# Channel-major LayerNorms, an early query product and gates broadcast through DRAM in a conv, attention and mixture-of-experts kernel

## What is computed

```python
# conv block
y = depthwise_conv3x3(ln(x) @ inproj.T + b)          # ln over the 64 channels of a point
s = [y rows forward, backward, y columns forward, backward]      # 4 token orders
r = ln(s) @ ssm_in.T + b; a, g = split(r); u = a * sigmoid(g)
ys = nan_clean(conv1d_3taps(u) @ ssm_out.T + b) + s
x1 = nan_clean(mean_of_4_orders(ys) @ outproj.T + b) + x
# attention block, t = tokens of x1
xa = ln(t); q, k, v = split(xa @ W_qkv.T + b)        # 16 heads of 4 channels
k, v = head_ln(k), head_ln(v)
out = q @ (k.T @ v / 256)                            # per image and head
t2 = t + gelu((out + xa) @ W_proj.T + b) + xa
# mixture of experts: 8 experts, 64 -> 256 -> 64, the two best are weighed by softmax
xf = ln(t2); w = softmax of the top two logits of xf @ Wg + bg
result = t2 + sum_e w[:, e] * (gelu(xf @ W1[e] + b1[e]) @ W2[e] + b2[e])
```

## Time and profile before

| | |
|---|---|
| median of 3 runs | 100.32 us (100.15 to 100.49) |
| the profiled execution's own time | 100.63 us |
| its span, first to last instruction | 98.9 us |
| busy PE, DVE, ACT, POOL | 87.7, 67.8, 55.1, 25.0 us |

### The profile page before, as it was taken

One profiled execution on the slowest core, in us unless ns is written; L12 is line 12 of the kernel. 1 busy time (PEld: TensorE's weight loads), 2 busy tenths in 40 slices (PEclk: granted clock), 3 DMA queues, 4 the chain that ended last, 5 costly groups with the idle time before them and its releaser, 6 DMA issues. The chain is left out here.

```text
span 98.9 us, 1512 instructions
## 1 busy us (share of the span) xinstructions
PE 87.7 (89%) x445; PEld 51.8 (52%) x445; DVE 67.8 (69%) x234; ACT 55.1 (56%) x112; POOL 25.0 (25%) x56
## 2 busy tenths in 40 slices
PE   3998999799999996998895999999999889999930
PEld 1346865544734353354452778664686554666510
DVE  1648769876665799586467747848889854822871
ACT  5264463997746582724655828939966502992000
POOL 6456000012223061100047300031242041630630
PEclk9999999999999999999999999999999999999998
DMA  1999400000000000000000000000000000010001
GB/s 45 246 383 401 199 0 0 3 0 7 0 0 0 3 0 0 0 0 0 0 0 0 0 7 3 0 3 0 0 0 0 7 0 0 0 53 0 0 0 53
DMA packets 1447, 3.49 MB, mean 35 GB/s; under 512 B 160, under 2 KB 800, under 8 KB 1312
## 3 DMA queue, kind: packets, MB, share of 16 engines
q1 hardware_dynamic: 1296, 3.32, 9.4%
q10 hardware_dynamic: 144, 0.09, 0.3%
HBM read 3.15 MB, written 0.26 MB: 34 GB/s over the span
## 5 line engine op out<-in xcount | busy, mean ns | idle before, releaser
L525 ACT ACTIVATE hs<-psA,early 128x512 f32<-128x512 f32 x16 | 11.0, 690 | 8.8 <-PE psA L795 8.4
L810 PE MATMUL psM<-hs,w_sb 128*64 128x256 f32 x128 | 15.4, 384 | 0.4 <-DVE prod L1197 0.4
L627 PE MATMUL psB<-warm 128*128 128x512 bf16 x45 | 13.9, 437 | 1.5 <-DVE warm L1226 1.5
L810 PEld LDWEIGHTS psM<-hs,w_sb 128*64 128x64 f32 x128 | 8.7, 136 | 5.2 <-DVE prod L1197 0.9
L525 ACT ACTIVATE hs<-psB,early 128x512 f32<-128x512 f32 x16 | 11.0, 690 | 0.0
L361 POOL TENSOR_TENSOR acc<-acc,prod 128x512 f32<-128x512 f32 x5 | 6.4, 1281 | 15.0 <-DVE prod L1197 15.0
L1197 DVE SCALAR_TENSOR_TENSOR prod<-psM,early,wbc 128x256 f32<-128x256 f32 x16 | 7.1, 480 | 4.4 <-PE psM L810 3.8
L627 PEld LDWEIGHTS psB<-warm 128*128 128x128 bf16 x45 | 5.1, 117 | 7.5 <-issue 3.9
L794 PE MATMUL psA<-xh,w_hl 128*128 128x512 f32 x16 | 7.3, 454 | 0.2 <-DVE xl L1118 0.2
L1187 DVE COPY wbc<-psT 128x512 f32<-128x512 f32 x8 | 5.5, 687 | 2.7 <-PE psT L833 2.7
L794 PE MATMUL psB<-xh,w_hl 128*128 128x512 f32 x16 | 6.3, 395 | 0.0
(11 more groups left out here) (204 smaller groups left out, 186.7 us busy)
## 6 DMA issues: line engine op xcount, KB each, us to landing
w_nat<-in_w_dram SPq DMA_DIRECT2D x1, 1024.0 KB, 7.8
late<-in_late_dram SPq DMA_DIRECT2D x1, 616.0 KB, 5.8
w_sb<-in_w_dram SPq DMA_DIRECT2D x1, 512.0 KB, 8.7
ssm_in<-in_ssm_dram SPq DMA_DIRECT2D x1, 320.0 KB, 4.2
x_tok<-in_x_tok_dram SPq DMA_DIRECT2D x2, 128.0 KB, 2.5
x_sb<-in_x_chan_dram SPq DMA_DIRECT2D x1, 256.0 KB, 7.9
out_dram<-fin SPq DMA_DIRECT2D x2, 128.0 KB, 1.7
early<-in_early_dram ACTq DMA_DIRECT2D x1, 89.5 KB, 2.7
```

What stands on the lines that cost most here:

```text
L525: nc.scalar.activation(hs[:, n % RING, :], hidden_bank(n), ACT.Gelu, bias=cols(V_B1 + n % (E * CK))).then_inc(S["h_ok"], 1)
L627: nc.tensor.matmul(psB[:, 0, :], warm[:, 0:P], warm[:, :], start=True, stop=True)
L810: m = nc.tensor.matmul(psM[q * C:(q + 1) * C, bank, c0:c0 + L], w2_sb[:, s % (E * CK), :], hs[:, s % RING, q * L:(q + 1) * L], start=(k == ...
```

## The change

All three channel-major norms (of x, y and x1) stay channel-major. A product with center (identity minus the mean over an image's 64 channels) gives the centered tile in psT, ACT squares it (center_squares), a product with mean_of gives the variance in each of the 256 columns (variance), ACT makes rstd for 128x256 elements, and DVE multiplies (normalise). For x the input weights are multiplied with center beforehand (z_w), and z_out scales the product by rstd. x_tok is no longer loaded; x_chan is, as two DMAs, in its place.

The ssm products of an image use only its own 64 partitions and put a and g of image 0 in psA and of image 1 in psB; gates, gated_u and raster go by image. Keys and values do the same with the two halves of the points; their bias goes in as three bf16 parts (kv_bias_parts). The query of all points is made early (query_product, query_out) from xa_c; heads is then applied to it (retrieval), xa_c added on DVE (with_query_input), and projection multiplies with the projection weights.

gate_parts ends after two instructions; gate_rows transposes float32, rows_out copies 16 x 256 numbers, SP writes them to DRAM (gate_mem), and reads them back in four DMAs that repeat each row over 64 partitions of wbc. spread_gates and spread_out are gone. Most lists are put in another order.

```diff
-            sp.dma_start(x_sb[:, :, :], a["x_chan"]).then_inc(S["xp_in"], 16)
+            def gates_to_all_channels(h):
+                sp.wait_ge(S["rows_ok"], h + 1)
+                sp.dma_start(gate_mem[h], gate_rows_sb[:, h, :]).then_inc(Q["rows_out"][h], 16)
+                sp.wait_ge(Q["rows_out"][h], 16)
+                for half in range(2):
+                    e0 = half * (E // 2)
+                    for q in range(2):
+                        rows = gate_mem[h, q * E + e0:q * E + e0 + E // 2, :]
+                        sp.dma_start(wbc[q * C:(q + 1) * C, h, e0:e0 + E // 2, :],
+                                     rows.unsqueeze(0).to_broadcast([C, E // 2, L]))\
+                            .then_inc(Q[f"wbc_in{half}"][h], 16)
...
+            def center_squares(n, h):
+                act.wait_ge(Q["cen_ps"][h], n + 1)
+                nc.scalar.activation(cen_sq[:, h, :], psT[:, h, 0:L], ACT.Square).then_inc(Q["sq_ok"][h], 1)
...
-                nc.scalar.activation(lnv[:, h, :], mv[:, h, :, 1], ACT.Ln, bias=eps).then_inc(Q["t_lnv"][h], 1)
+                nc.scalar.activation(lnv[:, h, :], psT[:, h, L:2 * L], ACT.Ln, bias=eps).then_inc(Q["t_lnv"][h], 1)
...
+                nc.tensor.matmul(psT[:, h, 0:L], center[:, :], src[:, h, :], start=True, stop=True)\
+                             .then_inc(Q["cen_ps"][h], 1)
...
+                nc.tensor.matmul(psT[:, h, L:2 * L], mean_of[:, :], cen_sq[:, h, :], start=True, stop=True)\
+                             .then_inc(Q["var_ps"][h], 1)
...
-                for g, bank in ((1, psB), (0, psA)):
-                    for q in range(2):
-                        m = nc.tensor.matmul(bank[:, h, q * L:(q + 1) * L], ssm_w[:, g, q, :], norm_c[:, h, :],
+                for g in (1, 0):
+                    for q, bank in enumerate((psA, psB)):
+                        rows = slice(q * C, (q + 1) * C)
+                        m = nc.tensor.matmul(bank[:, h, g * L:(g + 1) * L], ssm_w[rows, g, q, :], norm_c[rows, h, :],
...
+            def retrieval(h):
+                pe.wait_ge(S["heads_ok"], h + 1)
+                pe.wait_ge(S["query_ok"], h + 1)
+                nc.tensor.matmul(psA[:, h, 0:L], heads[:, h, :], query[:, h, :], start=True, stop=True)\
+                             .then_inc(S["ret_ps"], 1)
...
-                for g in range(2):
-                    pick = pick_q[:, 2 * i % E + g, :, :].rearrange("r q c -> r (q c)")
-                    m = nc.tensor.matmul(psT[:, h, g * L:(g + 1) * L], pick, w3T[:, h, :], start=True, stop=True)
-                m.then_inc(S["wbc_ps"], 1)
...
+                nc.vector.tensor_tensor(dst[:, h, :], psT[:, h, 0:L], rstd[:, h, :], ALU.mult)\
+                             .then_inc(Q["c_norm"][h], 1)
...
             def gated_pair(i):
-                spread_out(i)
                 gated(2 * i)
                 gated(2 * i + 1)
```

More of the change, by code:

```diff
@@ L836, in _ @@
-            pe.wait_ge(S["warm_ok"], 1)
-            keep_clock(9)
+                    m = nc.tensor.transpose(psT[0:2 * E, h, L + t * P:L + (t + 1) * P],
+                                            gates_t[:, h, t].rearrange("p q e -> p (q e)"), ident[:, :])
+                m.then_inc(S["rows_ps"], 1)
+            pe.wait_ge(S["warm_ok"], 1)
+            keep_clock(7, psB[:, 0, :])
+            centered(0, 0, x_sb)
+            z_weight_product()
+            centered(0, 1, x_sb)
+            variance(0, 0)
@@ L851, in _ @@
+            query_transpose()
+            centered(1, 1, y_sb)
+            variance(1, 0)
+            variance(1, 1)
+            keep_clock(3, psB[:, 0, :])
             ssm_products(0)
-            to_tokens(1, y_sb, "y_ok")
+            ssm_products(1)
+            keep_clock(2, psT[:, 1, :])
             raster(0)
-            to_channels(1, 1)
             column(0)
-            ssm_products(1)
+            raster(1)
             outproj(0)
-            keep_clock(1)
-            raster(1)
@@ L877, in _ @@
-            to_channels(2, 1)
-            keep_clock(2)
-            to_tokens(0, t2, "t2_ok")
-            keys_values(1)
-            keep_clock(8)
+            centered(2, 0, x1)
+            keep_clock(5, psT[:, 1, :])
+            variance(2, 0)
+            outproj(1)
+            keep_clock(1, psT[:, 1, :])
+            query_product(0)
+            keys_values(0)
+            keep_clock(2, psT[:, 1, :])
+            centered(2, 1, x1)
+            keep_clock(2, psM[:, 1, :])
+            variance(2, 1)
@@ L1248, in _ @@
             kv_weights()
-            w1_low(0)
+            gated_u(0, 0)
+            gated_u(0, 1)
+            gated_u(1, 0)
+            gate_low()
+            ln_weights()
+            gated_u(1, 1)
+            kv_bias_parts()
             clean_dirs(0, 0)
             clean_dirs(0, 1)
-            gated_u(1)
+            clean_dirs(1, 0)
             residual(0)
-            stats(2, 0)
-            normalise(2, 0)
-            w1_low(1)
-            clean_dirs(1, 0)
-            clean_dirs(1, 1)
@@ L1259, in _ @@
-            square_sums(0)
-            residual(1)
-            kv_scaled(0)
-            stats(2, 1)
-            head_matrix(0)
-            query_and_bias(0)
-            gate_low()
-            normalise(2, 1)
-            tokens_after_attention(0)
-            stats(3, 0)
-            square_sums(1)
-            normalise(3, 0)
-            kv_scaled(1)
+            clean_dirs(1, 1)
+            w1_low(0)
+            normalise(2, 0, xa_c)
+            residual(1)
+            square_sums(0, 0)
@@ L1272, in _ @@
+            square_sums(0, 1)
+            kv_scaled(0, 0)
+            kv_scaled(0, 1)
+            normalise(2, 1, xa_c)
+            head_matrix(0)
+            w1_low(1)
+            with_query_input(0)
+            square_sums(1, 0)
+            square_sums(1, 1)
+            tokens_after_attention(0)
+            stats(0)
+            kv_scaled(1, 0)
+            kv_scaled(1, 1)
+            normalised_copies(0)
+            head_matrix(1)
             token_low(0)
-            head_matrix(1)
@@ L1274, in _ @@
[L1274 removed]
+            with_query_input(1)
+            w1_low(2)
+            w1_low(3)
+            tokens_after_attention(1)
             largest(0)
             second(0)
[L1277 removed]
             gate_parts(0)
[L1279 to L1280 removed]
+            stats(1)
+            normalised_copies(1)
             rows_out(0)
[L1282 to L1283 removed]
+            token_low(1)
+            largest(1)
             gated_pair(0)
[L1285 removed]
```

586 lines of the change are left out of this document (274 added, 312 removed).

## The result

The changed kernel takes 95.53 us in the median of four runs (95.31, 95.40, 95.66 and one of 98.25 at a granted clock of 0.978); the kernel before, beside it, 100.23. The ratio is 0.952 (95% interval 0.948 to 0.957): faster by 4.8%. The forecast was 93.6, so 1.9 us of the gain are missing, of which this profiled execution (95.40, span 93.7) shows 1.5. The time lies in the whole range of 92.0 to 96.3, but outside the forecast's own of 92.4 to 94.6.

The account below looks back on a forecast made before the run. PE bounds the mixture stage; ahead of it a relay between PE, ACT and DVE decides. Start 3.7 earlier, length 2.0 and tail 1.0 less give 6.7 us: median 100.32 becomes 93.6, own range 92.4 to 94.6, whole range 92.0 to 96.3.

Parts of the forecast that it names:

- (a): Ssm stage: the two images' 64-partition products don't run side by side; 1.2 us stay, 94.8 us; chance 0.20.
- (b): Mixture: gate DMAs take longer than 6.2 us, each us beyond counting twice; 96.1 us at 7; chance 0.11.
- (d): Mixture: PE's clock falls after a 1.35 us wait; priced at 2 us, 95.6 us; chance 0.04.
- the relay: Short steps between PE, ACT and DVE ahead of the mixture; hidden(0) at 51.9, 3.7 us earlier.
- the gates' way: Row copy to wbc through DRAM: 5.3 us, between 4.7 and 6.4; pair 1 waits 1.35 us at output(12).
- (e): Norm of y: batching stalls pair 0, so the stages before the mixture gain nothing; 97.3 us; chance 0.06.
- One sign of being wrong: Mixture: the prediction is wrong if output(4) also waits for gates; up to about 6.2 us was free there.
- (c): Gate reads at w_nat's pace, 10 us: slower than before, 102.1 us, decisive from 9.1 on; chance 0.06.
- x1 of pair 1 at 37.05: End of the 1d convolutions: pair 1's x1 ready at 37.05 against 42.27, five microseconds won.
- The tail of 1.0: After the last output product only a product and the last sum follow: 1.0 us instead of 1.97.
- Each us counts twice: Mixture: every us of gate DMA time beyond 6.2 counts once for each pair.
- The two pieces of the gain: Mixture starts 3.7 us earlier; its length falls 2.0 and its tail 1.0 us.

Follow-up runs that it names:

- e1: Changed kernel with each pair's gate rows written to DRAM twice, reads waiting for both; median 100.26 us, ratio 0.997 to the kernel before.
- e4: Changed kernel with GpSimd doing bad_out(1) before attention_residual(0); median 96.54 us, ratio 0.955 to the kernel before.
- e10: Changed kernel with the ssm products over all 128 rows instead of 64; median 97.07 us, ratio 0.968 to the kernel before.
- e2: Changed kernel with pair 0's gate rows transposed after output(1) and copied out before normalised_copies(1); median 96.84 us, ratio 0.947 to the kernel before.
- e5: The changed kernel as it is, run again; median 95.68 us, ratio 0.953 to the kernel before.
- e9: Changed kernel with gates again spread by TensorE and the mixture order of the kernel before; median 96.63 us, ratio 0.962 to the kernel before.
- e6: Changed kernel with hidden(14) and hidden(15) moved ahead of output(12) on TensorE; median 94.33 us, ratio 0.938 to the kernel before.
- e3: Changed kernel with each half of the gates read by one DMA for all 128 partitions; 119.4 us, ratio 1.190 to the kernel before.
- e12: Changed kernel with both pairs' gate steps moved earlier, and hidden(14) and hidden(15) ahead of output(12); median 94.28 us, ratio 0.939 to the kernel before.

## Why the prediction was right, and where 1.9 us went

**Faster, within the whole range: right, but not within the forecast's own.** 95.53 is 0.9 above the 94.6 to which the forecast itself reached; the whole range held it because the prices of the rivals (a), (b) and (d) had widened it to 96.3. The order of the stages came out as worked out: the relay up to x1 of pair 0 gives nothing (31.48 against 31.67), pair 1's x1 comes 4.4 us earlier, and the gates' way is behind both waits of the mixture. Rivals (a) and (e) fell: the row tiles start 0.01 us apart, all 16 instructions are done in 2.0 us, and raster(0) was within 0.15 us of its step. One sign of being wrong did show: output(4) also waited for gates, 0.41 us, which is the beginning of rival (b). No run of the changed kernel came near (c), but it lay closer than the L of 9.1 that I had worked out, since a fallen clock adds to long waits: e1, at 7.7 and 7.9, is already at 0.997 of the kernel before.

**Between x1 of pair 0 and hidden(0), 0.9 us mis-sized.** The step "x1 of pair 1 at 37.05" measured 37.91. DVE's last cleaning ends 0.3 later than I had; the products and conv_out behind it put o_sb at 35.30 where I had 34.7; and the residual, with 0.37 for o_bad, took 0.3 more. That pair 1's lateness costs pair 0 the prediction has, with head_rstd behind pair 1's square (38.2): that square ended at 39.14, so kv_n ended at 41.15 and not 40.35, gelu_p at 45.88 and not 44.9. square_sums(0, ...), on DVE behind residual(1), were done at 38.56 and did not hold it. In e4 GpSimd's order didn't mend it.

**The gates' way L, "5.3, between 4.7 and 6.4".** From the end of the row copy to the first gated product it measured 6.4 us for pair 0 and 6.1 for pair 1 in the changed kernel, and 6.1 to 7.0 for pair 1 in eight other profiles with the same DMAs. The write took 1.4, less than my 1.7. The two issues ahead of the first half took 0.6 each, not 0.43, and the 512 KB landed 4.5 us after their first issue (4.8 in pair 0), where I had 0.43 and 3.1. The estimate by the Trainium skill (DMA: Bandwidth & Descriptors, section "Anatomy of one DMA"), 5.8, was closer, and its fixed part of 2.0 us is again above the write's 1.4. So the wait ahead of output(12) was 1.97 and not 1.35, and output(4) waited 0.41: L up to 5.95 was free there and not 6.2. How exactly the wait follows L shows in the profiles in which output(12) keeps its place behind output(11): for L of 6.07 (changed), 6.35 (e10), 6.59 (e2), 6.62 (e5), 7.01 (e4) and 7.93 (e1) the wait is 1.97, 2.26, 2.49, 2.53, 2.91 and 3.83, always 4.1 less. What makes L differ between executions of the same DMAs stays open. Against the longer waits, PE had 33.9 us of work from hidden(0) to its last product where I had 34.5: waits of 0.45, 0.41, 0.62 and 1.97 make 37.35, for 37.2 forecast.

**The tail of 1.0** is 1.38, from 90.16 to 91.54: DVE still had a sum of its own (L1240, 90.19 to 90.61) ahead of the last gated product, which the prediction left out. With 0.9 and 0.15 this makes the 1.4 us between 90.1 and 91.54. The remaining 0.4 lies between this execution and the medians.

**"Each us counts twice"** is right for a lengthened way (e1: 3.2 us more of waits, for ways that were 1.3 and 1.9 us longer). The reason is that output(4), the ring of 12 GELU tiles and the tanh of pair 1 stand in one line behind pair 0's gates. It does not hold the other way: e2 sent pair 0's rows almost 3 us earlier, and counted from hidden(0) pair 1's row copy came only 0.5 earlier.

**Rival (d) is what I weighed too lightly.** At 0.04 it was the least likely of the rivals, for a wait of 1.35. In the profile of the changed kernel the clock stays 1.00, as in e5's and e4's with 2.5 and 2.9 us of wait, but with 2.5 and 3.8 it fell in e2 and e1, and the changed kernel's runs at 0.965 and 0.978 are 4.3 and 2.7 us longer. That these two, one in six and one in four, come from this place is not shown, since neither left a profile.

**The two pieces of the gain** are both smaller than forecast: in the two profiles the mixture starts 2.8 us earlier, where I had 3.7, and is with its tail 2.45 shorter, where I had 3.0. e9 cuts the gain another way. All but the broadcast gives 3.8 there; the prediction's terms for it are 3.7 and, for the short products in the mixture, 0.8. The broadcast with its order gives 0.9, where 2.2 are left of the 6.7. So the broadcast fell shortest of its forecast, by 1.3; e6, which fills the wait at output(12), gives back 1.35.

## What to carry to other kernels

Replacing engine work by a round trip through DRAM pays only as far as something stands in front of it: look for work that doesn't need the data and put it into the wait (e6: one move, 1.35 us), before you try to shorten the trip. Compare the length of the trip, as it differs from execution to execution (here 6.1 to 7.0 us), with what it is hidden behind. Ask of each wait on PE what its clock does behind it, and of a multi-dimensional DMA what its slowest dimension is. A swap on one of two engines that read the same memory may only turn a wait into a longer instruction.

## What was not expected of the hardware

- A DMA of 512 KB with 2 as its slowest dimension ran at about 53 GB/s, where 64-partition reads of the same rows ran at 230 to 270 and loads at up to 418 (e3). Reads that repeat a DRAM row kept the DMA share at 0.96 to 1.00 at that rate, so it was not limited by missing work; why it is below the loads' was not tried.
- DVE instructions with SBUF inputs beside a running POOL addition took 0.85 us instead of 0.45 (128x256, e4), and 0.85 instead of 0.19 for pair 1's ld (128x32 at 73.88, POOL's sum from 73.40 to 74.68).
- The start varies between executions of the same code: raster(0) at 18.7 in one profile of the changed kernel (e5), 19.2 in the other, and 20.0 in e6 and e12, whose lists are the same up to there, and with it the time, by 1.3 us. The differences begin with PE's first products: the seven keep_clock ones take 3.03 us in e5 and 3.17 in the others, and then the pair of centering products 0.59, 0.81 and 1.06 us for the same two instructions, at a granted clock of 1.00 in every row. The cause stays open. From raster(0) to hidden(0), on the other hand, every kernel with the changed order takes 33.5 to 33.6 us, where the one before takes 35.8.
